# A gated cross-attention and FP4 feed-forward block: every engine's calls in another order

## The chip, the cores and the metric

The program runs on one core of a Trainium2 chip. The time is what the device takes for one execution, in microseconds (us). The engines are named as in the profile: PE multiplies matrices (PEld is its loading of weights), DVE is the vector engine, ACT the scalar engine, POOL the GpSimd engine, and SP only issues DMA transfers and waits for semaphores. Each engine has its own list of instructions and takes them strictly in order; engines meet only at semaphores.

## The reference

`x` is 8 batches of 512 rows of 512 numbers; `ctx` is 8 batches of 77 keys of 512. Cut to what matters:

```python
def xattn(k, v, q):                     # k = v = ctx, q = layernorm(x)
    kp = k @ Wk.T;  vp = v @ Wv.T + bv;  qp = q @ Wq.T + bq
    probs = softmax(qp @ kp.T / sqrt(512))
    return (probs @ vp) @ Wo.T + bo
def ffn(x):                             # w_gate, w_up: 1408 x 512, w_down: 512 x 1408
    gate = fp4(x) @ fp4(w_gate).T;  y = fp4(x) @ fp4(w_up).T
    return fp4(silu(gate) * y) @ fp4(w_down).T
x = x + tanh(g_xattn) * xattn(ctx, ctx, layernorm(x))
x = x + tanh(g_ffn) * ffn(layernorm(x))
```

`fp4` takes blocks of 16 numbers, divides by a scale (the block's largest magnitude over 6), rounds to the grid 0, 0.5, 1, 1.5, 2, 3, 4, 6 and multiplies back. It is applied to the three weight matrices, to every normalised row and to every hidden row.

## The kernel before

**Tiles.** The 4096 rows are 32 tiles `t` of 128 rows; four tiles make a batch `b`. The kernel splits each quantised number into a 16-bit high and low part, so a product of two quantised matrices is three 16-bit matmuls: high by high, high by low, low by high.

**Start (about the first 130 us).** Weights come in by DMA. Keys and values are folded into small products (`key_product`, `vo_product`, `value_product`). The gate and up weights come in eleven chunks `j`, the down weights in four `r`. A chunk goes through `gu_tops`, `gu_scales` (DVE), `gu_divide` (POOL), `gu_squares` (ACT), `gu_round` (two DVE instructions), `gu_times` (POOL), and is then turned and split, by PE and ACT for the first six chunks (`gu_turn`, `gu_high`, `gu_subtract`, `gu_low`) and by POOL, ACT and DMA transposes for the others (`gu_high_of`, `gu_low_of`, `move_gu`). The down weights do the same with names that begin `down_`.

**A tile's normalised rows.** `x_stats` (ACT, then POOL), `x_apply` (ACT), `x_scales`, `x_divide` (DVE), `x_squares` (ACT), `x_round` (DVE), `x_times` (POOL), `x_high` (ACT), `x_low` (DVE), and `x_turn`, a DMA transpose from SP into one of two buffers. Then PE can begin `gate_up(t, c, m)`: chunk `c` of the hidden width (512, 512 and 384 columns), `m` 0 for gate and 1 for up. Chunks alternate between two PSUM banks per matrix: chunk 2 of a matrix needs the bank of its chunk 0 to have been read.

**A tile's hidden rows.** `gate_silu` (ACT) and `hidden` (DVE) read the banks. Then, in two parts, `h_scales` (DVE), `h_divide` (POOL), `h_squares` (ACT), `h_round` (DVE), `h_times` (POOL), `h_high` (ACT), `h_low` (DVE) and `h_turn` (DMA transpose). PE does `down(t, g)` in three groups, `finish` (DVE) adds it to the rows and `store` writes them. `down` runs two tiles behind `gate_up`.

**Attention.** For the batch after the current one: `ln1_*`, `xn_apply`, `xn_high`, `xn_low`, `xn_turn`, then `att_scores` (PE), `softmax` (DVE), `exps`, `prob_high` (ACT), `prob_low` (DVE), `p_turn` (DMA), `att_values` (PE), `values` (DVE), once for each of the batch's four tiles `i`. The first two batches are turned by PE (`att_turn`, `prob_turn`) and not by DMA.

**What sets the order.** Nothing plans it at run time. Each engine's program is a list of calls: up to tile 6 every call is written out, and from tile 7 a loop over `t` issues one tile, with `attention_part(t, at)` putting the attention's calls at named places. A semaphore wait inside a call keeps the data right whatever the order; a call that waits holds everything behind it on its engine.

Of the kernel before, what the change touches and what calls it, by code (L numbers as in the profile page):

```python
# [15 lines left out]
P = 128  # L16
# [45 lines left out]
def build(nc, x, ctx_kv, g_xattn, g_ffn, Wk, Wv, bv, Wq, bq, Wo, bo, w_gate, w_up, w_down, out):  # L62
# [20 lines left out]
    with ctx:  # L83
# [359 lines left out]
        def sync_program(e):  # L443
# [47 lines left out]

            for r in range(KD):
                e.dma_start(stage_a[:, r, :], Wk[r * P:(r + 1) * P, :]).then_inc(loads[f"wkq{r}"], 16)
                e.dma_start(stage_b[:, r, :], Wq[r * P:(r + 1) * P, :]).then_inc(loads[f"wkq{r}"], 16)
                load_gu(r)
# [23 lines left out]
            load_down(3)  # L519
            for j in LAST_MOVED:  # L520
                move_gu(j)
# [43 lines left out]
            def turn_part(t, s):  # L565
                b = t // TILES + 1
                if CUT <= b < NBATCH and t % TILES == s:
                    xn_turn(b, 2 * s)
                    xn_turn(b, 2 * s + 1)

            def attention_part(t, at):
                b, s = t // TILES + 1, t % TILES
                if STACKED <= b < NBATCH:
                    if (s, at) == (1, "end"):
                        stack_values(b)
                    elif (s, at) == (2, "first"):
                        p_turn(b)

            def store(t):
                b, s = t // TILES, t // TILES % SLOTS  # L580
                w.wait_ge(x2_made, t + 1)
                e.dma_start(out_rows[b][:, t % TILES, :], x_tile(t)).then_inc(x_out[s], 16)
                if t % TILES == TILES - 1 and b + SLOTS < NBATCH:
                    w.wait_ge(x_out[s], 16 * TILES * (b // SLOTS + 1))
                    load_x(b + SLOTS)
# [7 lines left out]
            move_down(0)  # L593
            move_values(4)
            move_values(5)
            move_values(6)
            move_values(7)
            move_down(1)
# [3 lines left out]
            h_turn(0)  # L602
            w.wait_ge(h_div[1], 2)
            load_x(3)
            h_turn(1)
            x_turn(4)
            w.wait_ge(h_div[1], 3)
            load_x(2)
            h_turn(2)
# [4 lines left out]
            p_turn(2)  # L614
            h_turn(4)
            x_turn(7)
            h_turn(5)
            store(0)
            store(1)
            store(2)  # L620
            store(3)
            for t in range(7, NT):
# [3 lines left out]
                if t + 1 < NT:  # L626
                    x_turn(t + 1)
# [15 lines left out]
        def pool_program(e):  # L643
# [175 lines left out]
            for t in range(7, NT):  # L819
# [3 lines left out]
                if t < NT - 1:  # L823
                    x_times(t + 1)
# [1550 lines left out]
```

## Time and profile before

| | |
|---|---|
| median of three runs | 832.52 us (832.37 to 833.18) |
| span of the profiled execution | 832.3 us |
| PE busy | 822.4 us (99%), 4102 matmuls |
| DVE busy | 650.7 us (78%), 967 instructions |
| ACT busy | 459.9 us (55%) |
| POOL busy | 400.5 us (48%) |
| share of the chain that ended last | PE 93%, ACT 3%, DVE 2% |
| granted PE clock | full speed in all 40 slices |

The span is the time from the first to the last instruction of one profiled execution; it lies 0.2 us under the median. A matmul's end is modelled and contains the time that it takes to run through the array, so the row of a wait shows a little less idle time than PE really lost, and the start of one matmul to the start of the next is the exact measure. The timeline merges neighbours of one kind; "x8" is eight instructions, and "[1.20 <-ACT ...]" is idle time in front and what ended it.

### The profile page before, as it was taken

What the parts mean: (1) busy time and instruction counts of PE and PEld (TensorE: products, weight loads), DVE (VectorE), ACT (ScalarE), POOL (GpSimd) and SP (SyncE); (2) the same over time, 40 slices, a digit from 0 to 9 for tenths busy, and PEclk for the clock granted to TensorE, in tenths of its full rate; (3) what the DMA queues carried; (4) which work ended last, traced back from release to release, by engine and by line L of the source; (5) the groups of instructions that cost most, each with busy time, mean ns of one, the idle gap of its engine ahead of it and who ended that gap; (6) DMA issues with size and microseconds to landing.
All of it is one profiled execution on the core that took longest, in us unless ns stands there. A gap on an engine that the chain in (4) does not pass through costs nothing.

```text
span 832.3 us, 11653 instructions
## 1 busy us (share of the span) xinstructions
PE 822.4 (99%) x4102; PEld 417.0 (50%) x4102; DVE 650.7 (78%) x967; ACT 459.9 (55%) x930; POOL 400.5 (48%) x333
## 2 busy tenths in 40 slices
PE   9999999999999999999999999999999999999998
PEld 5555445444554445444544454445544454444445
DVE  5887899898998698877878688778876878776654
ACT  2778675547555666456563755366646565344320
POOL 3498797764334353444333543454444533444421
PEclk9999999999999999999999999999999999999999
DMA  9723703553243434532641255224433443222232
GB/s 318 285 70 103 157 13 97 122 128 92 48 80 106 108 82 89 129 56 54 114 120 40 55 110 136 61 60 99 97 61 61 85 85 73 58 54 55 48 75 73
DMA packets 192817, 78.21 MB, mean 94 GB/s; under 512 B 176387, under 2 KB 178037, under 8 KB 192759
## 3 DMA queue, kind: packets, MB, share of 16 engines
q1 hardware_dynamic: 192759, 77.47, 39.6%
q8 instruction: 32, 0.52, 0.2%
q14 instruction: 26, 0.21, 0.1%
HBM read 22.76 MB, written 8.39 MB: 37 GB/s over the span
## 4 chain that ended last, share of the span: by engine, by line
PE 93%; ACT 3%; DVE 2%; issue 1%; DMA 1%; POOL 1%; POOLq 0%; ACTq 0%; DVEq 0%
PE banks L1918 60%; PE banks L2037 27%; DVE banks L1417 1%; PE banks L2053 1%; PE banks L1912 1%; PE banks L1971 1%; PE banks L1999 1%; PE banks L1998 1%; PE banks L2143 1%; DMA x_T<-x_parts 1%; PE banks L2150 0%; PE banks L2008 0%; PE banks L2160 0%; PE banks L2165 0%; PE banks L2155 0%
## 5 line engine op out<-in xcount | busy, mean ns | idle before, releaser
L1918 PE MATMUL banks<-wgu_hi,x_T 128*128 128x512 f16 (+1 forms) x1536 | 439.3, 361 | 1.6 <-DMA x_T<-x_parts 0.9
L1918 PE MATMUL banks<-wgu_lo,x_T 128*128 128x512 f16 (+1 forms) x768 | 277.5, 361 | 0.0
L1918 PEld LDWEIGHTS banks<-wgu_hi,x_T 128*128 128x128 f16 x1536 | 150.3, 98 | 155.6 <-issue 1.3
L2037 PE MATMUL banks<-wd,arena 128*128 128x512 f16 x1023 | 227.2, 379 | 0.0
L2037 PEld LDWEIGHTS banks<-wd,arena 128*128 128x128 f16 x1023 | 99.7, 98 | 117.4 <-issue 0.6
L648 POOL TENSOR_TENSOR arena<-arena,h_r 128x1024 f32<-128x1024 f32 (+1 forms) x60 | 93.2, 1554 | 115.3 <-DVE h_r L1372 115.3
L648 POOL TENSOR_TENSOR arena<-arena,h_s 128x1024 f32<-128x1024 f32 x64 | 90.7, 1418 | 88.6 <-DVE arena L1419 53.6
L1918 PEld LDWEIGHTS banks<-wgu_lo,x_T 128*128 128x128 f16 x768 | 75.1, 98 | 76.8 <-issue 0.3
L648 POOL TENSOR_TENSOR xwork<-xwork,x_s 128x512 f32<-128x512 f32 x32 | 38.4, 1201 | 152.0 <-DVE xwork L1419 152.0
L1052 ACT ACTIVATE arena<-banks,scal 128x512 f32<-128x512 f32 (+1 forms) x96 | 61.9, 647 | 84.9 <-PE banks L1918 84.8
L1571 DVE SCALAR_TENSOR_TENSOR arena<-arena,scal,banks 128x512 f32<-128x512 f32 (+1 forms) x90 | 62.2, 694 | 56.3 <-PE banks L1918 53.5
L1417 DVE SCALAR_TENSOR_TENSOR arena<-arena 128x384 f32<-128x384 bf16 (+1 forms) x67 | 69.1, 1031 | 37.6 <-ACT arena L842 37.5
L1419 DVE SCALAR_TENSOR_TENSOR arena<-arena 128x384 f32<-128x384 bf16 (+1 forms) x67 | 65.7, 981 | 2.3
L842 ACT ACTIVATE arena<-arena 128x384 bf16<-128x384 f32 (+1 forms) x67 | 54.0, 805 | 20.0 <-POOL arena L648 19.9
L648 POOL TENSOR_TENSOR arena<-arena,valo 128x1024 f32<-128x1024 f32 x22 | 48.8, 2246 | 26.0 <-DVE valo L1372 22.4
L1064 ACT CAST h_parts<-arena 128x1024 f16<-128x1024 f32 x64 | 49.0, 770 | 15.3 <-POOL arena L648 15.3
L1591 DVE TENSOR_TENSOR h_parts<-arena,h_parts 128x1024 f16<-128x1024 f32 x64 | 57.4, 901 | 0.0
L957 ACT ACTIVATE xwork<-ring,shift,rstd 128x512 f32<-128x512 f32 x29 | 23.6, 813 | 56.3 <-POOL shift L694 56.2
L1367 DVE TENSOR_REDUCE h_s<-arena 128x64 f32<-128x1024 f32 (+1 forms) x60 | 52.6, 877 | 0.5
L1058 ACT CAST x_parts<-xwork 128x512 f16<-128x512 f32 x32 | 19.7, 617 | 54.4 <-POOL xwork L648 54.4
L842 ACT ACTIVATE xwork<-xwork 128x512 bf16<-128x512 f32 x29 | 18.2, 629 | 50.4 <-DVE xwork L1546 50.4
L1596 DVE SCALAR_TENSOR_TENSOR ring<-banks,scal,ring 128x512 f32<-128x512 f32 x31 | 23.1, 745 | 24.8 <-PE banks L2037 24.8
(199 smaller groups left out, 1043.6 us busy)
## 6 DMA issues: line engine op xcount, KB each, us to landing
ring<-in_x_dram SPq DMA_DIRECT2D x8, 1024.0 KB, 5.1
out_dram<-ring SPq DMA_DIRECT2D x31, 256.0 KB, 2.2
arena<-in_L_ffn_w_down_dram SPq DMA_DIRECT2D x4, 704.0 KB, 5.0
arena<-in_L_ffn_w_gate_dram SPq DMA_DIRECT2D x5, 512.0 KB, 9.7
arena<-in_L_ffn_w_up_dram SPq DMA_DIRECT2D x5, 512.0 KB, 9.6
ring<-in_L_xattn_Wk_dram SPq DMA_DIRECT2D x4, 256.0 KB, 6.1
ring<-in_L_xattn_Wq_dram SPq DMA_DIRECT2D x4, 256.0 KB, 6.8
wd<-in_ctx_dram SPq DMA_DIRECT2D x1, 1024.0 KB
```

The lines of the kernel that those rows point to most:

```text
L648: return e.tensor_tensor(blocks(dst), blocks(src), spread(s), ALU.mult)
L842: return e.activation(c, v, ACT.Square, scale=ROOT)
L957: e.activation(x_w(t), x_tile(t), ACT.Identity, bias=shift2[:, :], scale=rstd2[:, :]).then_inc(x_norm, 1)
L1052: e.activation(silu[par][:, 0:n], bank[par][:, 0:n], ACT.Silu, scale=p_gu).then_inc(silu_done, 1)
L1064: e.copy(h_parts[:, PARTS[i]], h_q[:, PARTS[i]]).then_inc(h_hi[i], 1)
L1367: e.tensor_reduce(s, blocks(src), axis=AX_X, op=ALU.max, apply_absolute_value=True).then_inc(*step())
L1417: e.scalar_tensor_tensor(between, square, FLOOR, v, ALU.add, ALU.add).then_inc(*step())
L1419: return e.scalar_tensor_tensor(to, square, FLOOR, between, ALU.add, ALU.subtract)
L1571: e.scalar_tensor_tensor(h_of(t)[:, c0:c0 + n], silu[par][:, 0:n], h_fold, bank[2 + par][:, 0:n], ALU.mult, ALU.mult).then_inc(h_made, 1)
L1591: e.tensor_tensor(h_parts[:, lo], h_q[:, PARTS[i]], h_parts[:, PARTS[i]], ALU.subtract).then_inc(h_lo[i], 1)
L1918: ended = e.matmul(at, l, r, start=(i == 0), stop=(i == len(terms) - 1))
L2037: ended = e.matmul(by_k(down_ps(t)[:, :], KD), l, r, start=(k == 0 and i == 0), stop=(k == KH - 1 and i == 2))
```

## The change

No call, buffer, shape or wait is added or taken away. On SP, POOL, ACT, DVE and PE the calls stand in another order, from the first tile to the last. The loop over one tile with `attention_part` goes; in its place stands a loop over four tiles (one batch `n`), with every call written out, and a written-out end for tiles 28 to 31. The reload of a batch's rows, which was part of `store`, is a call of its own. On PE, `ended.then_inc(bqk_turned, 1)` is written some lines later but still belongs to the same transpose instruction.

The core of it, first the start of ACT and of PE (in a long list, only the calls spoken of later):

```diff
 ACT
+            ln1_stats(0)
+            key_copy(1)
+            key_copy(2)
+            gu_folds(0, EARLY)
...
             wo_copy(0)
             wo_copy(1)
...
-            gu_folds(0, EARLY)
...
             gu_high(3)
+            gu_squares(7)
...
-            gu_folds(5, NPAIR)
-            gu_squares(7)
-            gu_squares(8)
...
+            down_squares(0)
+            down_squares(1)
+            gate_silu(0, 0)
             gu_low(11)
...
             x_high(1)
 PE
+            key_product(2)
+            key_product(3)
             wo_turn(2)
...
+            gate_up(0, 0, 0)
+            gu_subtract(11)
+            gate_up(0, 0, 1)
             value_product(4)
             gate_up(0, 1, 0)
             gate_up(0, 1, 1)
+            gate_up(0, 2, 0)
             att_turn(1, 0)
+            gate_up(0, 2, 1)
+            gate_up(1, 0, 0)
             att_turn(1, 1)
...
+            gate_up(2, 0, 1)
+            gate_up(2, 1, 1)
+            prob_turn(1)
             gate_up(2, 0, 0)
```

The same stretch on DVE and SP:

```diff
 DVE
             gu_round(6)
             gu_round(7)
             down_tops(0)
+            softmax(0)
             gu_round(8)
+            value_row()
             gu_round(9)
-            value_row()
-            softmax(0)
             sums(0)
             value_rows(0)
+            gu_round(10)
             values(0, 0)
-            gu_round(10)
...
             value_rows(3)
-            value_rows(4)
             down_round(0)
             down_round(1)
             x_low(1)
+            value_rows(4)
             hidden(0, 0)
...
             sums(1)
             x_round(3)
-            hidden(1, 2)
             hidden(2, 0)
+            values(1, 0)
             h_round(0, 0)
             x_low(3)
 SP
+            x_turn(0)
             for j in LAST_MOVED:
                 move_gu(j)
-            x_turn(0)
-            x_turn(1)
-            move_values(1)
             move_values(2)
-            x_turn(2)
             move_values(3)
             move_values(4)
             move_values(5)
+            move_values(1)
+            x_turn(1)
```

The new loop on PE, the new order on ACT, DVE and SP around the softmax, and on POOL at the very end:

```diff
 PE
+            for t in range(2 * TILES, NT - TILES, TILES):
+                n = t // TILES + 1
                 gate_up(t, 0, 0)
+                gate_up(t, 1, 0)
                 gate_up(t, 0, 1)
                 gate_up(t, 1, 1)
+                gate_up(t, 2, 1)
+                down(t - 2, 0)
                 gate_up(t, 2, 0)
+                att_scores(n, 0)
                 down(t - 2, 1)
+                gate_up(t + 1, 0, 0)
...
+                att_scores(n, 2)
+                att_scores(n, 3)
...
+                gate_up(t + 2, 0, 0)
+                gate_up(t + 2, 0, 1)
+                gate_up(t + 2, 1, 0)
+                down(t - 1, 2)
+                gate_up(t + 2, 1, 1)
+                att_values(n, 0)
+                att_values(n, 1)
+                gate_up(t + 2, 2, 1)
+                gate_up(t + 2, 2, 0)
...
 ACT
+                h_squares(t + 1, 0)
+                h_high(t, 0)
+                exps(n)
+                h_squares(t + 1, 1)
+                prob_high(n)
+                gate_silu(t + 2, 0)
+                x_apply(t + 3)
 DVE
+                h_low(t, 1)
+                h_low(t, 0)
+                softmax(n)
+                h_round(t + 1, 0)
+                h_round(t + 1, 1)
+                x_scales(t + 3)
+                prob_low(n)
+                sums(n)
+                hidden(t + 2, 0)
 SP
+                x_turn(t + 2)
+                p_turn(n)
+                h_turn(t)
 POOL
+            h_divide(31, 0)
+            h_times(31, 0)
+            h_divide(31, 1)
+            h_times(31, 1)
```

Before, PE took the scores of a batch in its tile `t + 1` and the values in tiles `t + 2` and `t + 3`, and DVE took `prob_low` at the end of tile `t + 1`, more than a tile ahead of the first `att_values`.

## Rows read from the trace of the kernel before

**Rows 1.** Busy us by stretch: PE, PEld, DVE, ACT, POOL; clock, DMA share.

```profile
0.00:130.00 130.00, 122.84 (x489) 69.11 (x490) 104.64 (x132) 85.88 (x170) 93.01 (x63) 1.00 0.50 154
130.00:285.15 155.15, 155.15 (x797) 79.79 (x795) 135.32 (x202) 90.19 (x177) 80.29 (x64) 1.00 0.45 101
...
462.96:832.30 369.34, 366.57 (x1899) 181.07 (x1897) 270.50 (x417) 180.12 (x367) 149.18 (x135) 1.00 0.35 74
```

**Rows 2.** Chain that ended last, of one period of four tiles: start, us, what.

```profile
395.44 2.59 PE banks L1918 x12
...
411.32 7.12 PE banks L2037 x33
418.45 14.26 PE banks L1918 x72
```

**Rows 3.** Timeline of PE near 38 us: start, us, what, idle before.

```profile
38.50 1.13 PE L1912 MATMUL banks<-ident,ring 128*128 128x128 f32 x8 [1.20 <-ACT valo L1128]
```

**Rows 4.** Timeline of DVE: a rounding of weights in the start.

```profile
61.94 2.34 DVE L1417 SCALAR_TENSOR_TENSOR banks<-x_T,arena 128x1024 f32<-128x1024 bf16 x1 [3.07 <-ACT x_T L842]
```

**Rows 5.** Timeline of DVE: x_low(0), three value_rows, a down rounding, x_low(1).

```profile
98.60 0.68 DVE L1554 TENSOR_TENSOR x_parts<-xwork,x_parts 128x512 f16<-128x512 f32 x1
...
109.21 2.06 DVE L1669 SCALAR_TENSOR_TENSOR ring<-banks,scal,h_parts 128x512 f32<-128x512 f32 x3
...
116.16 1.62 DVE L1417 SCALAR_TENSOR_TENSOR arena<-arena 128x1408 f32<-128x1408 bf16 x1 [0.69 <-ACT arena L842]
...
119.36 3.08 DVE L1554 TENSOR_TENSOR x_parts<-xwork,x_parts 128x512 f16<-128x512 f32 x1
```

**Rows 6.** Timeline of POOL beside the last of them.

```profile
118.54 6.36 POOL L648 TENSOR_TENSOR arena<-arena,h_parts 128x1408 f32<-128x1408 f32 x2 [0.70 <-ACT h_parts L878]
```

**Rows 7.** Timeline of PE: three waits, the last before tile 1's first matmul.

```profile
119.25 1.27 PE L1912 MATMUL banks<-ident,xn 128*128 128x128 f32 x8 [0.28 <-ACT xn L947]
...
123.16 0.34 PE L1918 MATMUL banks<-wgu_hi,x_T 128*128 128x384 f16 x1 [0.69 <-DVE arena L1571]
...
127.06 0.38 PE L1918 MATMUL banks<-wgu_hi,x_T 128*128 128x512 f16 x1 [0.93 <-DMA x_T<-x_parts]
```

**Rows 8.** DMA transposes, issue to landing: x_T, then h_T, then p_T.

```profile
DMA to landing us min/median/max: 3.0/3.2/4.5
...
DMA to landing us min/median/max: 5.2/5.3/7.0
...
DMA to landing us min/median/max: 2.8/2.8/4.3
```

**Rows 9.** Timeline of the SP queue: the transpose of tile 3.

```profile
157.09 1.23 SPq L526 DMA_TRANSPOSE x_T<-x_parts  x1
```

**Rows 10.** Timelines of DVE and PE: softmax, prob_low, x_scales, first values of one batch.

```profile
591.62 0.44 DVE L1467 SCALAR_TENSOR_TENSOR prob<-banks,scal,keyb 128x308 f32<-128x308 f32 x1
...
598.37 0.48 DVE L1509 SCALAR_TENSOR_TENSOR xn<-prob,xn 128x308 f16<-128x308 f32 x1 [2.84 <-ACT xn L1031]
...
600.49 0.68 DVE L1367 TENSOR_REDUCE x_s<-xwork 128x32 f32<-128x512 f32 x1
...
601.61 0.35 DVE L1542 RECIPROCAL x_r<-x_s 128x32 f32<-128x32 f32 x1
...
610.35 0.38 PE L1998 MATMUL banks<-valo,xn 128*128 128x512 f16 x1
```

**Rows 11.** Timeline of ACT in that batch: x_apply, exps, gate_silu.

```profile
594.36 0.81 ACT L957 ACTIVATE xwork<-ring,shift,rstd 128x512 f32<-128x512 f32 x1 [3.19 <-POOL shift L694]
595.19 1.28 ACT L984 ACT_TABLE_LOAD   x1
596.49 1.11 ACT L984 ACTIVATE prob<-prob,neg_top 128x77 f32<-128x77 f32 x4
...
600.18 0.69 ACT L1052 ACTIVATE arena<-banks,scal 128x512 f32<-128x512 f32 x1
```

**Rows 12.** Timeline of the SP queue: the last hidden tile's four transposes.

```profile
817.05 5.28 SPq L538 DMA_TRANSPOSE arena<-h_parts  x4
```

More of the change, by code:

```diff
@@ L1324, in scalar_program @@
             h_squares(5, 1)
+            key_high(1)
+            key_high(2)
+            x_stats(8)
+            key_back(0)
+            key_back(1)
             gate_silu(6, 2)
+            gate_silu(7, 0)
             h_high(5, 0)
+            key_high(3)
             h_high(5, 1)
-            key_high(0)
-            key_high(1)
-            x_stats(8)
             h_squares(6, 0)
             x_apply(8)
-            for t in range(7, NT):
+            h_squares(6, 1)
+            key_back(2)
@@ L1334, in scalar_program @@
+            x_squares(8)
+            gate_silu(7, 1)
+            x_stats(9)
+            h_high(6, 0)
+            x_high(8)
+            ln1_sums(3)
+            gate_silu(7, 2)
+            h_high(6, 1)
+            x_apply(9)
+            h_squares(7, 0)
+            ln1_squares(3)
+            key_back(3)
+            for t in range(2 * TILES, NT - TILES, TILES):
+                n = t // TILES + 1
                 h_squares(t - 1, 1)
+                x_stats(t + 2)
+                value_high(n)
+                xn_apply(n, 0)
@@ L1345, in scalar_program @@
[L1345 to L1358 removed]
+                xn_high(n, 1)
@@ new lines, in scalar_program @@
+                xn_apply(n, 2)
+                h_squares(t, 0)
+                xn_high(n, 2)
+                xn_apply(n, 3)
+                x_apply(t + 2)
+                gate_silu(t + 1, 0)
+                gate_silu(t + 1, 1)
+                xn_high(n, 3)
+                h_squares(t, 1)
+                x_stats(t + 3)
+                x_squares(t + 2)
+                gate_silu(t + 1, 2)
+                h_high(t, 1)
+                x_high(t + 2)
+                h_squares(t + 1, 0)
+                h_high(t, 0)
@@ new lines, in scalar_program @@
+                exps(n)
[3 more added lines that the diff above has]
+                x_apply(t + 3)
+                x_squares(t + 3)
+                gate_silu(t + 2, 1)
+                x_high(t + 3)
+                x_stats(t + 4)
+                h_high(t + 1, 0)
+                x_apply(t + 4)
+                gate_silu(t + 2, 2)
+                x_stats(t + 5)
+                h_squares(t + 2, 0)
+                h_squares(t + 2, 1)
@@ new lines, in scalar_program @@
+                if n + 1 < NBATCH:
+                    ln1_sums(n + 1)
+                h_high(t + 1, 1)
+                gate_silu(t + 3, 0)
+                x_squares(t + 4)
+                gate_silu(t + 3, 1)
+                h_high(t + 2, 1)
+                if n + 1 < NBATCH:
+                    ln1_squares(n + 1)
+                h_high(t + 2, 0)
+                x_high(t + 4)
+                gate_silu(t + 3, 2)
+                h_squares(t + 3, 0)
+                x_apply(t + 5)
+            x_stats(30)
@@ new lines, in scalar_program @@
+            h_squares(27, 1)
+            h_high(27, 0)
+            gate_silu(28, 0)
+            x_squares(29)
+            gate_silu(28, 1)
+            x_high(29)
+            gate_silu(28, 2)
+            x_apply(30)
+            x_stats(31)
+            h_high(27, 1)
+            h_squares(28, 0)
+            h_squares(28, 1)
+            h_high(28, 1)
+            gate_silu(29, 0)
+            x_squares(30)
+            h_high(28, 0)
+            gate_silu(29, 1)
+            x_high(30)
@@ new lines, in scalar_program @@
+            gate_silu(29, 2)
+            x_apply(31)
+            h_squares(29, 0)
+            h_squares(29, 1)
+            gate_silu(30, 0)
+            x_squares(31)
+            h_high(29, 1)
+            gate_silu(30, 1)
+            x_high(31)
+            gate_silu(30, 2)
+            h_squares(30, 0)
+            h_high(29, 0)
+            gate_silu(31, 0)
+            h_squares(30, 1)
+            h_high(30, 0)
+            gate_silu(31, 1)
+            h_high(30, 1)
+            gate_silu(31, 2)
@@ L1795, in vector_program @@
             x_low(4)
+            values(1, 3)
             hidden(3, 1)
-            hidden(3, 2)
             h_round(2, 1)
@@ L1800, in vector_program @@
             finish(0)
-            values(1, 3)
             finish(1)
+            h_low(2, 1)
+            hidden(3, 2)
             h_low(2, 0)
-            h_low(2, 1)
             h_round(3, 0)
@@ new lines, in vector_program @@
+            h_round(27, 1)
+            finish(25)
+            x_scales(29)
+            hidden(28, 0)
+            x_divide(29)
+            x_round(29)
+            x_low(29)
+            hidden(28, 1)
+            h_low(27, 0)
+            h_scales(28, 0)
+            hidden(28, 2)
+            h_scales(28, 1)
+            h_low(27, 1)
+            finish(26)
+            h_round(28, 0)
+            h_round(28, 1)
+            x_scales(30)
+            x_divide(30)
+            x_round(30)
@@ new lines, in vector_program @@
+            hidden(29, 0)
+            hidden(29, 1)
+            h_low(28, 0)
+            x_low(30)
+            h_scales(29, 0)
+            hidden(29, 2)
+            h_scales(29, 1)
+            h_round(29, 0)
+            h_round(29, 1)
+            h_low(28, 1)
+            x_scales(31)
+            x_divide(31)
+            hidden(30, 0)
+            x_round(31)
+            finish(27)
+            x_low(31)
+            hidden(30, 1)
+            h_scales(30, 0)
+            h_low(29, 1)
@@ new lines, in vector_program @@
+            hidden(30, 2)
+            h_scales(30, 1)
+            h_low(29, 0)
+            h_round(30, 0)
+            h_round(30, 1)
+            hidden(31, 0)
+            h_low(30, 0)
+            h_low(30, 1)
+            hidden(31, 1)
+            finish(28)
+            h_scales(31, 0)
+            hidden(31, 2)
+            h_scales(31, 1)
+            h_round(31, 0)
+            h_low(31, 0)
+            h_round(31, 1)
+            h_low(31, 1)
+            finish(29)
+            finish(30)
@@ L2353, in tensor_program @@
+            down(30, 1)
+            down(30, 2)
             down_last()
```

990 lines of the change are left out of this document (481 added, 509 removed).

## The prediction

> **What bounds the kernel now.** I read the busy time by stretch first [rows 1]. Between 130.00 and 285.15 us PE's busy time equals the stretch, and in the last stretch only 2.8 of 369.3 us are missing (369.34 - 366.57), which is the tail after the last matmul. In the first 130 us 7.2 are missing (130 - 122.84), 1.5 of them before PE's first matmul. The granted clock is 1.00 in all three. Then the chain of waits in the steady part [rows 2]: it stays on PE alone, 14.26 us for a tile's `gate_up` (a chunk of 512 columns 2.59), 7.12 for a tile's `down`, one behind the other. So the reader sees a kernel bound by the sum of its matmuls from 130 us on. No matmul goes; a new order can take away only waits, and those all lie before 127 us. A matmul's end is modelled, so I also took PE's lost time from start to start over all of its matmuls: 11.3 us in all, every one before 127 us. The largest are 1.3 us in front of 38.50 [rows 3], and 0.45, 0.86 and 1.09 in front of the three instructions of [rows 7], where the rows say 0.28, 0.69 and 0.93. The ceiling of the change is thus some 8 to 11 us. What it can lose has no such ceiling, as in the steady part every late operand is paid on PE in full.
>
> **The change part by part.** *The start, to about 90 us.* ACT takes `gu_folds(0)` before `wo_copy(0)`. It waits for DVE's power of the gate and up weights (about 41 us), and behind it stand `wo_copy(0..3)` and `ln1_apply(0)`; PE's `wo_turn(2)`, at 38.50 before [rows 3], starts at about 42.1. Bounds: +3.6 us, if PE is what tile 0 waits for, and 0, if it is the chain of DVE, POOL and ACT over the weight chunks. I take 0, since PE has `key_product(2)` and `(3)` in front of it now and further waits behind it, which take up the lag. `gu_squares(7)` stands some 4 us earlier on ACT, so DVE's 3.07 us idle before the rounding at 61.94 [rows 4] go. `softmax(0)` in front of `gu_round(8)` now waits for PE's scores and gives most of it back. By my walk DVE is through with `gu_round(10)` 2.9 us earlier; 1.6 are left at `x_scales(1)`, and on PE about 1.0 of the waits of this stretch goes. Bounds for that term: 0 and 5 us (what PE loses before 110 us and after its first matmul, less the waits that nothing here touches); I take 1.0, as DVE's lead is what the chunks' turns follow and only part of it arrives.
>
> *Tile 1.* `x_low(1)` ended at 122.44 (119.36 + 3.08) [rows 5]. In the new order `value_rows(4)` stands behind it (-0.7, a third of the 2.06 at 109.21), `down_squares(0)` and `(1)` go together, so the 0.69 idle at 116.16 goes, and `x_low(1)` itself should take what `x_low(0)` took, 0.68 in place of 3.08 (-2.4), as POOL's 6.36 us pair `down_times(0)`, `(1)` [rows 6] can start only once its `down_round` is done, right about when `x_low(1)` starts. Of the 1.6 at `x_scales(1)` I keep 0.8, since `down_round(0)` still waits for POOL and ACT. Sum 4.6: `x_low(1)` ends at about 117.9. The transpose lands 3.2 us later in the median, 4.5 at worst [rows 8]: 121.1 to 122.4. PE comes to `gate_up(1, 0, 0)` at about 122.4 by itself, with one turn and one score less in front of it. So the wait of 1.09 goes, the 0.86 for `hidden(0, 0)` goes (that is DVE's next call, over 3 us earlier), and the 0.45 for ACT goes: 2.4, with the 1.0 from before 3.4 us of lead.
>
> *Tiles 2 and 3.* PE takes `gate_up(2, c, 1)` before `(2, 0, 0)`, so `gate_silu(2, 0)` comes late and `hidden(2, 0)`, now in front of `h_round(0, 0)` and `x_low(3)` on DVE, holds them. `x_turn(3)` was issued at 157.09 [rows 9]; in the new order it lands at about 159.3 where PE, which runs ahead, wants it at 158.8. -0.5. What stands behind it on SP, `h_turn(0)` and `h_turn(1)`, is in time by a us. Bounds: 0, and -2 if `values(1, 0)`, also new in front of `x_low(3)`, waits. I take the walk's 0.5.
>
> *The steady loop.* PE's work is the same, and by my walk over one batch no operand is late, but the margins are narrow: 1.4 us at `x_turn(t + 1)`, 2.0 at `x_turn(t + 2)`, 0.6 to 1.1 at the third `xn_turn`, 2.8 and 1.6 at the two `h_turn`s, and 1.3 to 1.9 at `p_turn`. The last is where most is given away: before, `prob_low` stood at 598.37 and the first `att_values` at 610.35 [rows 10]. Now, from the end of `att_scores(n, 3)`, the chain is `softmax` (first instruction 0.44, about 1.4 in all), ACT's table load 1.28, then 3.69 from the start of `exps` to that of `gate_silu` (596.49 to 600.18, `prob_high`, a part's squares and the second load within), `gate_silu` 0.69, `x_apply` 0.81 [rows 11], `x_scales` 1.47 (600.49 to 601.96) and `prob_low` 0.48 [rows 10], and the landing 2.8 [rows 8]: 12.6 us. PE has two groups of `down` (4.75), three chunks (7.77), one group (2.37) and one chunk (2.59) in between [rows 2], 17.5. Of the 4.9 between them some 3 to 3.6 go to handovers between engines, to `h_low(t, 0)` in front of `softmax`, and to `h_squares(t + 1, 1)`, which stands between `exps` and `prob_high` and waits for POOL. Cost taken: 0; bounds 0 and +15 (3 us in each of five batches), no gain possible since PE has no idle time here.
>
> *The end.* The last tile's part 1 is divided on POOL only after part 0 was multiplied. SP's last transposes went out in 5.28 us from 817.05 [rows 12]; the last one now goes out at about 821.7 and lands at 824.7 to 825.1, and PE needs it at 825.0. Cost 0 to 0.5; 0.2 taken.
>
> *Sum.* 3.4 - 0.5 - 0.2 = 2.7 us off the profiled execution's 832.3 gives 829.6; that execution lay 0.2 under the median of the runs, so 829.8.
>
> **A rule of the skill against it.** The row shows `x_low(1)`, which reads two operands in SBUF, at 3.08 us beside POOL's multiplications and 0.68 without [rows 5, 6]. The Trainium skill, "SBUF — State Buffer", section "SBUF: two separate sides", says that such a DVE instruction and a GpSimd one that reads SBUF exclude each other for a whole instruction, and whichever starts first has the port. By that rule my forecast hangs on which of the two starts first after `down_round(0)`; the result of the other case is the first rival's.
>
> **Rivals.** *The lead is eaten.* POOL's `down_times(0)` starts at about 117.5 and `x_low(1)` at 117.2; if POOL is 0.3 us earlier, or DVE later, `x_low(1)` waits for one of the two multiplications, 3.2 us (half of 6.36), and ends at about 121.4, lands at 124.6, and PE loses 2.2: 832.0. For it speaks that this is what happened before; against it that `down_times(0)` needs `down_round(0)`'s semaphore and DVE goes from one call to the next. A lag of 2 us at tile 3, or the 3.6 us of ACT's start reaching tile 0, ends in the same place, 831 to 833.
>
> *More is gained.* If DVE's 2.9 us arrive whole, PE loses little in the start beyond its first wait, and about 5.5 go: 827. Against it: PE's waits before 110 us are many and small, on several engines.
>
> *Slower.* The probabilities come late. The place is `p_turn(n)` in front of `att_values(n, 0)`; it decides once the chain of 12.6 us is more than 1.3 to 1.9 us later than in my walk. From then on each us is paid five times (n = 3 to 7), and a late PE does not catch up. With `prob_low` behind `x_scales(t + 3)`, and this behind `x_apply` and POOL's sums (ACT waited 3.19 for them once [rows 11]), 3.3 us late is possible: 1.7 paid each, 5 x 1.7 - 2.7 = +5.8, about 838. For it: the narrow margin and the long chain over four engines, two table loads in it. Against: it was no wait at all in the walk, and `x_stats(t + 3)` has been moved to well before.
>
> **How the numbers follow.** Forecast as it stands, 828.3 to 830.8, chance 0.49. More gained, about 827: 0.08. Lead eaten, 831 to 834: 0.25. Slower, 834.3 to 842, about 838: 0.18. A measurement of this kernel tells 0.2% (1.7 us, so outside 830.9 to 834.2) from no change. Faster by more: 0.49 + 0.08, less 0.02 for the forecast's upper edge, 0.55; slower by more 0.18; within 0.27. The predicted time is 829.8; the range 826.8 to 834.5 leaves out most of the slower case and little else.
>
> **What would show it.** Right: PE's idle in front of tile 1's first matmul gone and `x_low(1)` at about 0.7 us, ended near 118; tile 1 begun 3 to 4 us earlier, counting the turn and the score that moved behind it; no idle on PE between 165 and 820 us; `att_values(n, 0)` without a wait. The step for ACT's start is right if PE's `wo_turn(2)` is some 3.6 us late and tile 0's first matmul is not. Wrong: a wait of PE on `p_T` or on `xn_T` five times over (the slower rival, or its twin at the third scores), `x_low(1)` over 2 us with a POOL multiplication in front of it (lead eaten), a wait on `x_T` at tile 3 above 1 us, or more than 1 us after the last `finish` (the end).

## The result, and the profile after

The changed kernel takes 836.81 us (median of 4 runs, 836.70 to 837.57) against 832.68 for the kernel before (4 runs): ratio 1.005, 95% interval 1.0035 to 1.0064. It is slower by 4.1 us, outside the range of the prediction and on the other side of its sign.

Where a run's time and its span are both known, the time is 1.8 us above the span (836.86 and 835.0 here; 14 runs of before: median 833.03, spans 830.7 to 832.7, median 831.2). So the span of 832.3 that the prediction took for 832.5 us belonged to an execution of 834.1 us. Measured span against usual span, the change costs 835.0 - 831.2 = 3.8 us; against the traced execution 2.7.

PE's lost time from start to start (the start of one matmul to the start of the next, less what the earlier one usually takes), summed over all matmuls by stretch, shows where. Stretches and sums are in us; the second row is one more trace of before:

| | 0-45 | 45-95 | 95-112 | 112-130 | 130-285 | 285-835 | sum |
|---|---|---|---|---|---|---|---|
| before | 3.64 | 4.61 | 0.15 | 2.60 | 0.23 | 0.04 | 11.27 |
| before, again | 3.83 | 4.22 | 0.15 | 2.91 | 0.22 | 0.04 | 11.37 |
| changed | 5.94 | 0.46 | 6.08 | 0.01 | 0.05 | 1.61 | 14.14 |

About 0.5 us of the difference in the first stretch is not the change's. Up to 8 us both kernels do the same, and in every trace their first matmuls start at half rate (those of 128x128 in fp32 0.213 us apart in place of 0.111), though the clock's row reads 1.00 there. The full rate comes at 6.7 us in the first trace, 5.5 in the second, 7.6 in that of the changed kernel, and costs 2.3, 1.7 and 2.8 us.

Busy time by stretch of the changed kernel, columns as in [rows 1]; the last line is a short stretch by itself:

```profile
0.00:130.00 130.00, 121.48 (x478) 68.67 (x479) 105.74 (x129) 85.23 (x169) 87.46 (x59) 0.99 0.52 162
130.00:285.15 155.15, 155.15 (x803) 80.47 (x802) 135.11 (x203) 94.04 (x187) 78.77 (x67) 1.00 0.38 81
...
106.60:110.30 3.70, 3.65 (x11) 1.63 (x12) 3.60 (x8) 2.49 (x5) 2.17 (x1) 0.54 0.14 43
```

PE was busy 17.00 us of 17 between 95 and 112 before. Now its timeline there has one pause, and behind it matmuls that take 0.63 in place of 0.38 us and start 0.43 apart in place of 0.216:

```profile
98.78 3.60 PE L2068 MATMUL banks<-wd 128*128 128x512 f32 x8
106.65 0.58 PE L2104 MATMUL banks<-scal,ones 1*128 1x1 f32 x2 [4.27 <-DVE scal L1488]
107.16 0.61 PE L2087 MATMUL banks<-wgu_hi,neg_ident 128*128 128x512 f16 x1
107.56 0.63 PE L2068 MATMUL banks<-wgu_hi,x_T 128*128 128x512 f16 x1
...
110.51 0.59 PE L2068 MATMUL banks<-wgu_hi,x_T 128*128 128x512 f16 x2
```

The reader sees `value_product(3)`, then `power_spread('d')` waiting 4.4 us (start to start) for DVE's power of the down weights, then tile 0 at a granted clock of 0.54 in that stretch: mostly the lower level, 1.2 GHz, up to 110.0. That costs 1.5 us more (6.08 less the 4.43 of the pause and the 0.15 that this stretch lost before). The chain that ended last, over the pause (start, us, what):

```profile
98.50 2.51 DVE h_parts L1463
101.04 0.04 DVE h_parts L1465
101.08 0.58 issue
101.66 0.64 DVE x_s L1460
102.30 0.03 issue
102.33 2.13 DVE x_s L1633
104.48 0.04 DVE x_r L1635
104.52 0.23 issue
104.75 0.65 DVE ring L1705
105.40 0.66 DVE ring L1625
106.06 0.20 DVE scal L1484
```

Two small DVE instructions, of `down_scales(1)` and `x_scales(1)`, take 2.6 and 2.1 us (the chain counts 2.51 of the first). The first one's twin on another part of the weights, at 97.02, takes 0.20. The timelines of DVE and POOL have the reason:

```profile
98.42 2.59 DVE L1463 TENSOR_SCALAR h_parts<-h_parts 128x88 f32<-128x88 f32 x1
98.04 2.90 POOL L657 TENSOR_TENSOR arena<-arena,h_parts 128x1408 f32<-128x1408 f32 x1 [1.11 <-DVE h_parts L1465]
101.82 2.59 POOL L657 TENSOR_TENSOR arena<-arena,h_parts 128x1408 f32<-128x1408 f32 x1 [0.88 <-DVE h_parts L1465]
```

Each of the two DVE instructions ends within 0.1 us of a `down_divide` on POOL (98.04 + 2.90, 101.82 + 2.59). They have one operand in SBUF, not two. The change itself put the first one there. Before, DVE took `down_scales(0)` and `(1)` one behind the other, and both were through before POOL's pair began:

```profile
99.20 0.20 DVE L1370 TENSOR_SCALAR h_parts<-h_parts 128x88 f32<-128x88 f32 x1
100.05 0.14 DVE L1370 TENSOR_SCALAR h_parts<-h_parts 128x88 f32<-128x88 f32 x1
100.21 5.13 POOL L648 TENSOR_TENSOR arena<-arena,h_parts 128x1408 f32<-128x1408 f32 x2 [2.21 <-DVE h_parts L1372]
```

Now `x_low(0)` stands between them, POOL starts its first division at 98.04 while `x_low(0)` runs, and `down_scales(1)` comes behind it.

In the loop there are two more pauses, in one batch each: 0.9 us at the third scores of n = 3, and 0.6 at the first values of n = 5.

```profile
323.57 0.24 PE L2121 MATMUL banks<-keyq,xnT 128*128 128x154 f16 x1 [0.74 <-DMA xnT<-xn]
...
520.31 0.39 PE L2148 MATMUL banks<-valo,xn 128*128 128x512 f16 x1 [0.46 <-DMA xn<-xn]
```

The DMA view of the second (517 to 521.5 us in 40 slices of 0.11 us): behind the transpose of the probabilities, issued at 515.80, the queues move 0 to 11 GB/s for 14 slices (1.6 us), one instruction fetch (q8) is in flight, and the transpose lands after 4.5 us in place of 2.7.

```profile
DMA  9999980000001010000999999999999999999999
GB/s 330 262 273 269 137 7 0 0 0 0 0 0 9 7 11 9 9 9 11 200 291 289 285 258 278 271 246 212 214 228 223 209 228 212 218 205 225 221 223 205
...
q8 instruction: 1, 0.02, 1.8%
...
xn<-xn SPq DMA_TRANSPOSE x1, 4.5
```

### The profile page after: what moved, and what is told of

Read it like the earlier page. It is cut to its first block, busy times and chain, and to the rows that moved or that the text cites. A ratio compares the mean times of both kernels' runs of the same rounds, so it can differ in the third digit from the quotient of the medians.

```text
span 835.0 us, 11647 instructions
## 1 busy us (share of the span) xinstructions
PE 822.6 (99%) x4102; PEld 417.7 (50%) x4102; DVE 683.8 (82%) x967; ACT 458.3 (55%) x930; POOL 378.8 (45%) x333
## 4 chain that ended last, share of the span: by engine, by line
PE 85%; DVE 5%; SPq 4%; DMA 3%; issue 2%; ACT 1%; POOL 0%; DVEq 0%; ACTq 0%; POOLq 0%
PE banks L2068 55%; PE banks L2187 25%; SPq L455 1%; DMA arena<-in_L_ffn_w_up_dram 1%; PE banks L2203 1%; PE banks L2158 1%; PE banks L2062 1%; DMA arena<-in_L_ffn_w_down_dram 1%; PE banks L2148 1%; PE banks L2149 1%; DVE banks L1510 1%; PE banks L2074 1%; DMA xn<-xn 1%; DMA xnT<-xn 1%; PE banks L2121 0%
## 5 line engine op out<-in xcount | busy, mean ns | idle before, releaser
L2187 PE MATMUL banks<-wd,arena 128*128 128x512 f16 x1023 | 231.3, 379 | 0.0
L657 POOL TENSOR_TENSOR arena<-arena,h_r 128x1024 f32<-128x1024 f32 (+1 forms) x60 | 95.9, 1598 | 118.5 <-DVE h_r L1465 118.5
L657 POOL TENSOR_TENSOR arena<-arena,h_s 128x1024 f32<-128x1024 f32 (+1 forms) x64 | 95.7, 1506 | 70.5 <-DVE arena L1512 53.1
L657 POOL TENSOR_TENSOR xwork<-xwork,x_s 128x512 f32<-128x512 f32 x32 | 34.8, 1086 | 153.8 <-DVE xwork L1512 153.7
L1684 DVE TENSOR_TENSOR h_parts<-arena,h_parts 128x384 f16<-128x384 f32 (+1 forms) x64 | 79.9, 1258 | 18.5 <-ACT h_parts L1115 18.5
L1510 DVE SCALAR_TENSOR_TENSOR arena<-arena 128x384 f32<-128x384 bf16 (+1 forms) x67 | 70.3, 1049 | 7.1 <-ACT arena L893 7.1
L1512 DVE SCALAR_TENSOR_TENSOR arena<-arena 128x384 f32<-128x384 bf16 (+1 forms) x67 | 67.4, 1006 | 2.3
L1115 ACT CAST h_parts<-arena 128x1024 f16<-128x1024 f32 (+1 forms) x64 | 49.0, 768 | 35.2 <-POOL arena L657 21.7
L1647 DVE TENSOR_TENSOR x_parts<-xwork,x_parts 128x512 f16<-128x512 f32 x32 | 28.5, 889 | 14.5 <-ACT x_parts L1109 14.4
L1510 DVE SCALAR_TENSOR_TENSOR xwork<-xwork 128x512 f32<-128x512 bf16 x29 | 23.1, 796 | 8.7 <-ACT xwork L893 8.5
## 6 DMA issues: line engine op xcount, KB each, us to landing
arena<-in_L_ffn_w_gate_dram SPq DMA_DIRECT2D x5, 512.0 KB, 10.1
```

The source lines that it names most:

```text
L657: return e.tensor_tensor(blocks(dst), blocks(src), spread(s), ALU.mult)
L1115: e.copy(h_parts[:, PARTS[i]], h_q[:, PARTS[i]]).then_inc(h_hi[i], 1)
L1510: e.scalar_tensor_tensor(between, square, FLOOR, v, ALU.add, ALU.add).then_inc(*step())
L1512: return e.scalar_tensor_tensor(to, square, FLOOR, between, ALU.add, ALU.subtract)
L1647: e.tensor_tensor(x_parts[:, D:2 * D], x_q, x_parts[:, 0:D], ALU.subtract).then_inc(x_lo, 1)
L1684: e.tensor_tensor(h_parts[:, lo], h_q[:, PARTS[i]], h_parts[:, PARTS[i]], ALU.subtract).then_inc(h_lo[i], 1)
```

## The experiments

All times are medians in us, each with the ratio to before (95% interval); before, measured beside each, was 832.8 to 833.4.

**The two halves.** `start_new` keeps the changed lists up to tile 7 and takes the remaining calls in the order of before; `steady_new` is the reverse, before's lists up to tile 6 and then the new order.

> The changed kernel up to tile 7, and from the loop on every engine's remaining calls in the order of before. Theory (the loss lies in the start: PE waits 4.3 us at 106.65 for the down weights' power, then runs its next matmuls at half the granted clock, 1.2 us): PE's lost time to 140 us stays 12.4 us against 10.9 before, so this kernel is 1.5 us over before plus whatever lies outside the span (the changed kernel's runs are 1.8 us over their span); the two single waits of the new loop (0.9 and 0.6 us) are gone: span about 833.5, time 834 to 835.5. Rival (the new loop costs it, slower rival of the prediction): equal to before within 0.5 us.

> Before up to tile 6, and from there the calls in the changed kernel's order. Theory (start): only the loop's waits for a late landing, 0.9 us at one batch's third scores and 0.6 us at one batch's first values: span 832.3 + 1.5 = 833.8, time 833 to 834.5. Rival (the loop costs most of the 4 us): 836 or more, with a wait in several batches.

`start_new`: 836.93, 1.0043 (1.003 to 1.0056). `steady_new`: 835.33, 1.0026 (1.0016 to 1.0036). The start costs the most, as expected, but more than expected: here the pause was 5.1 us and the clock stayed low until 113, which cost some 2.8 us. The loop costs 2.3 us, where the changed kernel's trace has 1.6, with the same two pauses at 1.1 us each, and no others. The two halves thus cost 6.2 us by themselves and 4.1 together; most of the surplus is these longer pauses and the longer low clock. The pauses of `steady_new`:

```profile
321.11 0.24 PE L2917 MATMUL banks<-keyq,xnT 128*128 128x154 f16 x1 [0.94 <-DMA xnT<-xn]
...
518.36 0.39 PE L2944 MATMUL banks<-valo,xn 128*128 128x512 f16 x1 [0.97 <-DMA xn<-xn]
```

**The pause at the power.** `power_early` moves one call on DVE, `product_first` one on PE:

```diff
 power_early, DVE
             x_low(0)
+            power_of('d', pow_d)
             down_scales(1)
             x_scales(1)
             value_rows(1)
             values(0, 3)
-            power_of('d', pow_d)
 product_first, PE
             value_product(3)
+            value_product(4)
             power_spread('d', pow_d)
...
             gate_up(0, 0, 1)
-            value_product(4)
```

> The changed kernel with one DVE call moved: power_of('d') directly behind x_low(0), ahead of down_scales(1), x_scales(1), value_rows(1) and values(0, 3). Theory (PE waits because the power stands behind two small DVE instructions that POOL's multiplications hold for 2 us each): the power is made at about 99.8 in place of 106.6, PE's wait of 4.4 us and the 1.2 us at half clock go: 5.6 less, 831.2, if nothing else is late. Rival (another operand of tile 0 or tile 1 is late by as much, x_low(1) at 121.3 above all: PE's own arrival at tile 1 moves from 126 to about 120.5 while x_T lands at 124.6): only 1.5 to 2 us gained, 835.

> The changed kernel with one PE call moved: value_product(4) (3.43 us of matmuls) ahead of power_spread('d'), as before. Theory: the wait shrinks from 4.4 to about 1.0 us, and with so short a pause PE's granted clock doesn't fall: 3.4 + 1.2 = 4.6 less, 832.2; if the clock falls all the same, 833.4. Rival (tile 1 is late anyway): 835.

`power_early`: 835.81, 1.0037 (1.0024 to 1.005), near its rival's 835. `product_first`: 839.09, 1.0074 (1.0061 to 1.0086), slower than anything I had named. Both theories of mine failed, and the PE timelines (the first is `power_early`) say why: behind the wait for the power stood others on the same DVE calls.

```profile
102.24 0.39 PE L2087 MATMUL banks<-wgu_hi,neg_ident 128*128 128x512 f16 x1
105.42 0.39 PE L2068 MATMUL banks<-wgu_hi,x_T 128*128 128x512 f16 x1 [2.79 <-DVE ring L1705]
```

```profile
106.28 5.38 PE L2068 MATMUL banks<-wd 128*104 128x512 f32 x8 [3.58 <-DVE ring L1625]
```

`gate_up(0, 0, 0)` needs the bank that `value_rows(1)` reads, and `value_product(4)` one that `values(0, 3)` reads; both stand behind the two held instructions. The two held instructions themselves still take 1.80 and 2.12 us in `power_early`. In `product_first` the slow clock moreover fell on wide 32-bit matmuls (5.4 us for 3.6). `rows_early` moves `power_of('d')` and `value_rows(1)` both.

> The changed kernel with two DVE calls moved: power_of('d') and value_rows(1) directly behind x_low(0), ahead of down_scales(1) and x_scales(1). Theory (PE's 4.4 us wait had two releasers, one behind the other: the power at 106.6 and the bank that value_rows(1) frees for gate_up(0, 0, 0) at 105.4, both behind small DVE instructions that POOL holds for 2 us each): both waits go and with them the half clock. What is late next is tile 1: PE would come to gate_up(1, 0, 0) at about 120.5, x_low(1) still ends at about 121 and lands at 124.5, so 4 us are lost there: 2 us less than the changed kernel, 835. Rival (tile 1 is not late, since DVE's calls all come earlier too): 5.6 us less, 831.2.

833.42, 1.0006 (0.9997 to 1.0015): 3.4 us less than the changed kernel, with 95 to 112 us losing 0.15 as before. So the calls behind the two held ones were what the pause and its clock hung on. The next pause is 2.0 us, in front of `att_turn(1, 0)`:

```profile
121.99 0.66 PE L2062 MATMUL banks<-ident,xn 128*128 128x128 f32 x4 [1.84 <-DVE ring L1705]
```

In 9 executions at full mean clock the median is 833.3, in 2 with 0.998 or less it is 836.5. The trace is of one of the two, and its clock is low from 123.3 to 126.7, behind that pause.

**What is late next.** Each kernel adds to the one before it, on the full changed kernel (`x1_early`, `mended`, `mended_hidden`, `mended_act`) or with before's order from tile 8 (`joined`, `joined_turn`, `joined_both`).

```diff
 x1_early, joined:  DVE + x_low(1) ahead of down_round(0); ACT x_high(1) ahead of down_squares(0)
 mended, joined_turn:  PE att_turn(1, 0) behind gate_up(1, 0, 0)
 mended, loop:  DVE prob_low(n) ahead of x_scales(t + 3); SP stack_values(n) behind xn_turn(n, 2)
 joined_both:  PE key_product(2) ahead of top_turn('gu')
 mended_hidden:  DVE hidden(0, 0) ahead of down_round(0)
 mended_act:  ACT gate_silu(0, 1) ahead of ln1_apply(1), xn_copy(1, 0) ahead of down_high_of(0);
              PE att_turn(1, 0) ahead of gate_up(1, 0, 0)
```

> As rows_early, and x_low(1) on DVE ahead of down_round(0) and (1), with gate_silu(0, 0), gu_low(11) and x_high(1) on ACT ahead of down_squares(0) and (1). Theory: x_low(1) at about 115, landing at 118, so tile 1 is not waited for: 5.6 us less than the changed kernel, 831.2, of which the new loop's 1.6 to 2.3 us are still paid. Rival (another wait, att_turn(1, 0) or the down weights, takes its place): 833 to 835.

> x1_early up to tile 7 and the order of before from there. Theory: the loop's two waits (1.1 us each as measured alone) go as well: 829.3, 3.5 us faster than before, which is the 45 to 95 us stretch's 4.1 us less what the first 45 us lose more. Rival (x1_early's start has another wait): 831 to 833.

> The changed kernel with all repairs: power_of('d') and value_rows(1) early on DVE, x_low(1) ahead of down_round(0), x_high(1) ahead of down_squares(0), att_turn(1, 0) on PE behind gate_up(1, 0, 0), and the two swaps in the loop. Theory (the changed kernel loses 4.4 us at the power, 1.3 at half clock, then 2.2 in front of att_turn(1, 0), which waits for ln1_apply(1) and that for down_round(0), and 1.6 to 2.3 in the loop; all else of it is better than before): 830.5 to 831.2, some 2 us faster than before. Rival (a wait of about 2 us appears elsewhere in tiles 1 to 3): 833.

> joined (the mended start, before's order from tile 8) with att_turn(1, 0) on PE behind gate_up(1, 0, 0). Theory: the wait of 1.7 us in front of it goes and with it those runs in which the clock falls: 831.0, and the spread of runs narrower. Rival (the clock falls for the waits near 32 us): the median stays at 832.3 or above with mean clocks of 0.998 and less in half of the runs.

> joined_turn with key_product(2) on PE back ahead of top_turn('gu'), as before. Theory (the first 45 us lose 5.3 against 3.7 before because PE waits there 1.3 us for the weights' largest value with key products left to do): about 0.8 us less than joined_turn, 830.2. Rival (the chunks' chain behind power_spread('gu') sets the pace, and what PE does while it waits is worth nothing): equal to joined_turn.

> mended with hidden(0, 0) on DVE ahead of down_round(0), down_round(1) and value_rows(4). Theory (gate_up(0, 2, 1) waits 2.4 us for the bank that hidden(0, 0) reads, and in a third of the executions the clock falls behind that pause): the wait goes, mean clock 1.00 in nearly all executions, 829 to 829.5, over 3 us faster than before. Rival (the next call in the row, hidden(0, 1) or att_turn(1, 0) behind ln1_apply(1), is late by as much): 831.5 to 832.5.

> mended_hidden with gate_silu(0, 1) ahead of ln1_apply(1) and xn_copy(1, 0) ahead of down_high_of(0) on ACT, and att_turn(1, 0) ahead of gate_up(1, 0, 0) on PE. mended_hidden loses 0.9 us for gate_silu(0, 1), 1.4 for a copy of a turned tile and 1.5 for another. Theory (a chain of single late calls): most of these 3.8 us go, 830 or less. Rival (DVE and ACT are at their limit between 95 and 135 us, so each repair only uncovers the next late call): 832.5 to 833.5, as mended and mended_hidden.

| | us | ratio, interval | full mean clock: runs, median | below: runs, median |
|---|---|---|---|---|
| x1_early | 834.19 | 1.0015 (1.0003-1.0026) | 5, 833.3 | 7, 835.3 |
| joined | 832.95 | 0.9999 (0.9991-1.0008) | 4, 831.7 | 7, 833.1 |
| mended | 832.22 | 1.0001 (0.9988-1.0014) | 6, 832.0 | 5, 833.9 |
| joined_turn | 833.58 | 1.0004 (0.9994-1.0014) | 4, 831.9 | 7, 834.0 |
| joined_both | 834.64 | 1.0022 (1.001-1.0035) | 2, 832.2 | 9, 835.1 |
| mended_hidden | 833.17 | 1.0002 (0.9993-1.0011) | 7, 832.9 | 5, 833.9 |
| mended_act | 833.56 | 0.9997 (0.9988-1.0007) | 3, 832.2 | 8, 833.7 |

None is faster than before; the theories had named 829 to 831.2, and the times are nearer the rivals' 831 to 835. Each repair moved the pause to the next call. PE timelines of `joined`, `mended` and (two lines) `mended_act`:

```profile
119.88 0.66 PE L2727 MATMUL banks<-ident,xn 128*128 128x128 f32 x4 [1.57 <-DVE ring L2100]
```

```profile
120.00 0.34 PE L2068 MATMUL banks<-wgu_hi,x_T 128*128 128x384 f16 x1 [2.21 <-DVE arena L1664]
```

```profile
121.88 0.66 PE L2062 MATMUL banks<-ident,xn 128*128 128x128 f32 x4 [0.91 <-DVE ring L1705]
...
133.18 1.19 PE L2068 MATMUL banks<-keyq,xnT 128*128 128x77 f32 x5 [2.00 <-ACT xnT L1030]
```

In `mended_act` DVE is busy 22.54 of the 24 us from 108 to 132. The time is about the one that the rival of the last expectation named. Its reason, engines at their limit, is not shown: before, DVE was busy 22.83 us of the same stretch with no pause of PE over 1.1, and the longest pause of `mended_act` ends with a copy on ACT, which was busy 18.30. That no order at all could do it is not shown either. `joined_both` was a plain miss: `key_product(2)` ahead cost 1 us in place of gaining 0.8, so the some 2 us that the changed start loses more than before ahead of 45 us are not explained by these key products. Some 0.5 us are the later full rate at the start; ACT's part of that stretch wasn't tried, and the rest stays open.

**The loop's two pauses.** `loop_swapped` is `steady_new` with the two loop swaps alone.

> steady_new (before's start, the changed kernel's loop) with two swaps in the loop: on DVE prob_low(n) ahead of x_scales(t + 3), on SP the two late xn_turns ahead of stack_values(n). Theory (the loop costs 2.3 us through two single waits, each behind a transpose that lands 1.6 us late while an instruction fetch is in the DMA queues, at a place with less than 1.6 us of slack): prob_low comes 2.8 us earlier and the last xn_turn 3.1 us earlier, both waits go, 833.0 as before. Rival (the loop is slower for another reason, or the late landing only moves to another operand with little slack): 834 to 835.5.

832.70, 1.0001 (0.9992 to 1.001), full clock in all 11 runs, and PE loses 0.05 us from 285 us on (2.3 in `steady_new`). The calls moved are those in front of the two transposes: the probabilities' transpose of that batch now goes out at 510.51, 6.7 us ahead of its first values at 517.25, where the changed kernel had 4.5 (515.80 to 520.31), wait included. In this trace it lands after 2.7 us, and the late landings (up to 4.4 for the same kind, in a batch ahead of the loop) met transposes that nobody waited for. But one of 5.0 us, the longest in `steady_new`, would have been in time too. So slack at two transposes was the whole price of the loop.

**The price of the clock.** `after_filled` put useless matmuls into `power_spread('d')`; `after_bridged` computes `value_product(3)` twice:

```diff
 after_bridged, PE, value_product(r)
+                if r == 3:
+                    product(bank[b][0:rows, 0:D], [...])
                 product(bank[b][0:rows, 0:D], [...]).then_inc(val_mm, 1)
```

> The changed kernel with 30 matmuls of 128 columns that nobody reads (identity by identity, into the bank that power_spread('d') has just taken), ahead of its wait for the power: about 3.2 us of work inside the pause of 4.4 us. The power comes when it came. Theory (the pause of 4.4 us makes the granted clock fall, and the matmuls behind it pay 1.3 us): the clock stays at full, PE's next matmuls have a pitch of 0.216 us in place of 0.43, and the kernel is 1.3 us faster than the changed one, 835.5. Rival (the slow matmuls come from something else, such as x_T or weights not being there): no change, 836.8; if the added matmuls delay PE, over 837.

> The changed kernel with value_product(3) computed twice on PE (the second time over the first, 3.43 us of matmuls, semaphore after the second), ahead of the wait for the power, which still comes at about 106.6. Theory (the pause of 4.4 us makes the granted clock fall): the pause is 1.0 us, the clock stays at full, the matmuls behind it have a pitch of 0.216 in place of 0.43, and though PE does 3.4 us more work the kernel is 1.3 us faster than the changed one: 835.5, mean clock 1.00. Rival (the slow matmuls have another cause, or the fall comes with the start of tile 0 whatever the pause): 836.8, clock 0.998.

`after_filled`, 842.59, 1.0118 (1.0105 to 1.0131), does not do what was meant: the bank that its matmuls take is freed by the power itself, so they ran behind the pause (8.6 us of them), not in it. It shows one thing only: the low clock (108.1 to 111.5) fell on these matmuls, and the tile's behind them have their 0.216 us again, so it is not the tile that is slow. `after_bridged`: 834.49, 1.0019 (1.0005 to 1.0032). With 3.4 us more work on PE it is 2.3 us faster than the changed kernel, a us more than expected, and in 6 of 11 executions the mean clock is 1.000 (834.4; the other five 836.4, and where their clock fell no trace shows). By the two traces 1.0 us of this lies between 95 and 112 (1.6 us lost and 3.4 of added work, for 6.1 lost) and 0.7 in the loop, where this trace met shorter waits; only the first can be the clock's:

```profile
98.93 7.03 PE L2068 MATMUL banks<-wd 128*128 128x512 f32 x16
107.38 0.38 PE L2104 MATMUL banks<-scal,ones 1*128 1x1 f32 x2 [1.42 <-DVE scal L1488]
...
107.92 0.38 PE L2068 MATMUL banks<-wgu_hi,x_T 128*128 128x512 f16 x1
```

**Before, again.**

> The kernel before, unchanged, for a second trace. Theory (the trace of before that the prediction rests on is of an execution 1.2 us above the usual, because x_low(1) met a POOL multiplication in it): the span is about 831.1, x_low(1) takes 0.68 us in place of 3.08, and PE does not wait for x_T in front of tile 1. Rival (the difference lies elsewhere, spread): x_low(1) takes 3 us again.

My theory fell: span 832.4, time 834.18, and `x_low(1)` takes 3.08 us again (first line, DVE). It isn't always so; in the trace of `steady_new`, with the same start (second fence), it takes 0.68 and PE has no wait for x_T in tile 1:

```profile
119.19 3.08 DVE L1554 TENSOR_TENSOR x_parts<-xwork,x_parts 128x512 f16<-128x512 f32 x1
```

```profile
119.27 0.68 DVE L2116 TENSOR_TENSOR x_parts<-xwork,x_parts 128x512 f16<-128x512 f32 x1
```

POOL's `down_times(0)` began at 118.37 in the one and at 119.35 in the other: the race of the first rival is real, and in the kernel before it is lost at least sometimes. Both traces of before are of slower executions (its spans run from 830.0 to 833.2), and so is the one of `loop_swapped` (3.08 again, at 832.0 the longest of its 11 spans). That fits a loss of a good us for each lost race. It isn't the only thing that varies: the full rate at the start came between 4.7 and 7.6 us in the 18 traces, at a cost of 1.4 to 2.8. A trace of a quick execution of before, which would settle it, I don't have.

## Why the prediction was wrong

**The bound.** Right: PE is the bound from 130 us, a lost operand is paid in full, all gain could only come from the start.

**The start, 1.0 us on PE.** Mis-sized both ways. 45 to 95 us gained 4.1, and the first 45 us lost 2.3, where I had 0 for ACT's `gu_folds(0)`; `wo_turn(2)` came at 40.79, 2.3 late and not 3.6 [rows 3]. Of the 2.3 some 0.5 are the start's half rate, and how much is that call is not shown. Together a gain of 1.9 where I took 1.0.

**The failed step is in "Tile 1", at its front.** It has PE arrive at `gate_up(1, 0, 0)` at 122.4 "by itself"; PE came there at 127.1, its wait for the power in front. On PE `value_product(4)` had moved from ahead of `power_spread('d')` to behind `gate_up(0, 0, 1)`, and I gave this move no price. Before, 7.03 us of products covered DVE's way from the turned maxima to the power, of which 3.6 were left:

```profile
100.94 7.03 PE L1918 MATMUL banks<-wd 128*128 128x512 f32 x16
```

Nor did I put PE's lead (its turn of the maxima 2.2 us earlier, 98.67 for 100.83) against DVE's `power_of('d')`, which had no such lead: before it was through at 104.3, now at 106.6. Price 4.4 us, and 1.5 for the clock. An estimate says what made the wait so long: with the two held instructions at 0.2 us each the power would have come 4.3 us earlier, at 102.3, and PE was ready for it at 102.2. So the wait needed both: with the shorter cover alone it would have been near nothing, and under the old cover (`product_first`) the held calls stopped PE at the next bank instead.

**The lock.** I weighed the Trainium skill's page "SBUF — State Buffer", section "SBUF: two separate sides", for `x_low(1)` alone. There the forecast held, 0.68 us with no POOL multiplication in front:

```profile
120.67 0.68 DVE L1647 TENSOR_TENSOR x_parts<-xwork,x_parts 128x512 f16<-128x512 f32 x1
```

And 112 to 130 us lose 0.01 in place of 2.60, but that is in part luck: `x_low(1)` ended at 121.35, not 117.9, since DVE was late by 4 us, and by 2.1 more in `down_round(0)`; x_T landed at 124.5, and PE didn't wait for it only because PE itself was 4.7 us late. At the forecast's 122.4 PE would have lost 2.1 us there, as the rival of the eaten lead has it. The same exclusion hit `down_scales(1)` and `x_scales(1)`, which I had walked at 0.2 and 0.7. The page also names DVE instructions in a two-port mode, which these one-operand ones can be. The mode stands in no trace, but the hold does, in all 18 of them (last section).

**The other terms.** Tile 3: 0.5 predicted, none measured. The end: 0.2 predicted, nothing measured (from the last 66 matmuls' start to the last instruction 10.1 us in both). The median: wrong by 1.6 us, as the trace was not of a usual execution; I had compared a span with times. The 2.7 us off the traced execution's 834.1 would have been 831.4; off the usual 833.0 they would be 830.3, if a usual execution had all of them left to gain.

**The slower rival.** Its place was right, `p_turn` and the third `xn_turn` (named as its twin), and its size wrong: it was paid once in each place and not five times, 1.6 us in this trace and 2.3 by itself, and its trigger is not the chain of four engines, which left about 1.1 us (515.80 and 2.7, for the values wanted at 519.7), near the 1.3 of the walk, but a landing 1.7 us over the median. I had the largest landing of [rows 8] in hand (4.3 for p_T) and used 2.8.

## What to carry to other kernels

When calls are reordered, follow each engine's lead to the first call that waits for an engine without that lead, and price moved waits even where the call itself takes 0.1 us. Compute slack with the longest landing in the trace, not the median. Look on every other engine for what a moved call now runs beside: here `x_low(0)` between two small calls let a long POOL instruction in. On a PE-bound kernel a pause can cost more than itself, because the clock behind it may fall; filling it with useless work was faster here.

## What the runs showed of the hardware

Small DVE instructions with one operand in SBUF (a `TENSOR_SCALAR` of 128x88 or 128x32) did not get past a multiplication on POOL. In the 18 traces 328 of them took more than 0.25 us, up to 2.59; every one had begun beside a POOL `TENSOR_TENSOR` and ended 0.03 to 0.07 us behind it. The 264 that met none took 0.24 at most, and so did 56 that began in its last 0.24 us. `RECIPROCAL` instructions of the same shapes took their 0.35 and 0.70 us beside POOL (192 of them) as without it.

The granted clock fell behind all five pauses of 2.9 us and more (up to 5.1). The work behind them lost some 1.5 us at the lower level, 2.8 in `start_new`. Below that the length of the pause alone does not decide: it fell behind 2.0, 2.2 and 2.4 us (`rows_early`, `mended_act`, `mended`) and not behind 2.2, 2.5 and 2.6 (`x1_early`, `joined_turn`, `joined_both`), nor behind several of 1.5 to 2.1. And it fell twice where no pause had been over 1.2 us: at 36.0 in `x1_early` (waits of 1.1 and 0.6 us ahead of it) and at 22.8 in `after_filled` (1.2). The same kernel can go either way: `rows_early` 833.3 us in 9 executions, 836.5 in 2.

DMA transposes land late beside instruction fetches (0.02 MB each). Of the transposes issued behind 130 us in the 18 traces, 1331 had no fetch between 0.5 us before their issue and their landing, and none of them landed more than 0.7 us over the median of its kind. 429 had one, and 130 of these did; the two behind the changed kernel's pauses by 1.5 and 1.7 us. What the fetch does to the transpose was not tested by itself.
